# The second attention's projection as three products of rounded parts, with rows turned two tiles at a time

## The reference

```python
x = x + _L0_xattn_ref(_layernorm(x), ctx_768, ...)                  # cross attention, 8 heads
x = x + _L0_ffn_ref(_layernorm(x), ...)                             # ternary weights, 8-bit tokens, gelu
x = x + _L1_xattn_ref(ctx_768, _layernorm(x), mask_BxS2_bk0, ...)   # the second attention
x = x + _L1_ffn_ref(_layernorm(x), ...)                             # 8 experts, the best 2, and a shared one

def _L1_xattn_ref(x, latents, mask, ...):       # latents: the normed tokens
    xn = layernorm(x, ln_x_g, ln_x_b)
    ln = layernorm(latents, ln_l_g, ln_l_b)
    q = ln @ Wq.T
    kv = jnp.concatenate([xn @ Wkv.T, ln @ Wlkv.T], axis=1)
    ...                                         # rms norm of q and k per head (4 heads of 64), softmax, values, Wo
```

## Time and profile before

| what | value |
|---|---|
| runs | 929.19, 927.93, 929.03 us; median 929.03 |
| profiled execution | 928.22 us, its span 926.5 us, mean granted clock 0.987 |
| busy | PE 94%, PEld 66%, DVE 68%, ACT 57%, POOL 42% |
| FFN's tail and projection | about 126 to 195 us of the span |
| second attention, then the experts | from 195 us to the end |

### The profile page before, as it was taken

One profiled execution on the slowest core, in us unless ns is written; L12 is line 12 of the kernel. 1 busy time (PEld: TensorE's weight loads), 2 busy tenths in 40 slices (PEclk: granted clock), 3 DMA queues, 4 the chain that ended last, 5 costly groups with the idle time before them and its releaser, 6 DMA issues.

```text
span 926.5 us, 14997 instructions
## 1 busy us (share of the span) xinstructions
PE 866.8 (94%) x4299; PEld 611.3 (66%) x4300; DVE 630.7 (68%) x1275; ACT 532.6 (57%) x851; POOL 388.9 (42%) x334
## 2 busy tenths in 40 slices
PE   9977789889999999999999999999999999999992
PEld 4635455545555555555457887878888888888881
DVE  5788987855567557456488779846666666666666
ACT  2558885445665765775554534326666666666650
POOL 2144455435676746756515545512222222222210
PEclk9999999989999999999999999999999999999997
DMA  9400000009478578569565100078711298526405
GB/s 310 110 1 1 0 1 1 1 5 364 160 292 328 194 305 326 219 269 350 199 262 196 82 1 1 12 316 342 305 40 36 71 348 341 208 88 254 116 9 182
DMA packets 49909, 154.07 MB, mean 166 GB/s; under 512 B 6266, under 2 KB 24438, under 8 KB 44236
## 3 DMA queue, kind: packets, MB, share of 16 engines
q1 hardware_dynamic: 46124, 144.25, 41.4%
q0 software_dynamic: 3744, 9.31, 3.1%
HBM read 97.85 MB, written 56.62 MB: 167 GB/s over the span
## 4 chain that ended last, share of the span: by engine, by line
PE 67%; DVE 17%; ACT 6%; issue 3%; DMA 3%; POOL 2%; SPq 1%; DVEq 0%; ACTq 0%; POOLq 0%
PE banks L1047 11%; PE banks L1300 8%; PE banks L1302 8%; PE banks L1301 8%; PE banks L1015 4%; PE banks L1039 3%; PE banks L1040 3%; DVE small L2105 2%; PE banks L1337 2%; PE banks L1339 2%; PE banks L1338 2%; PE banks L1313 2%; PE banks L953 2%; PE banks L919 1%; PE banks L1061 1%
## 5 line engine op out<-in xcount | busy, mean ns | idle before, releaser
L1047 PE MATMUL banks<-wexp 128*65 128x512 f32 (+1 forms) x288 | 149.9, 602 | 3.5 <-ACT wexp L1614 3.5
L677 POOL TENSOR_TENSOR cv_hl<-wexp,cv_hl 128x1024 fp32r<-128x1024 f32 x45 | 108.6, 2421 | 56.0 <-ACT cv_hl L1591 55.4
L1300 PE MATMUL banks<-ring,x_hi 128*128 x312 | 127.5, 408 | 0.0
L1302 PE MATMUL banks<-ring,x_lo 128*128 x312 | 122.1, 391 | 0.0
L1301 PE MATMUL banks<-ring,x_hi 128*128 x312 | 122.0, 391 | 0.0
L1614 ACT ACTIVATE wexp<-banks 128x512 f32<-128x512 f32 x128 | 76.4, 599 | 64.2 <-PE banks L1040 63.8
L2105 DVE TENSOR_REDUCE small<-banks 128x1 bf16<-128x1107 f32 x64 | 84.1, 1314 | 38.4 <-PE banks L1015 38.4
L1750 ACT ACTIVATE banks<-wexp 128x1024 f32 x72 | 73.5, 1021 | 47.7 <-DVE aux L2496 47.7
L1728 ACT ACTIVATE aux<-banks 128x512 f32<-128x512 f32 x78 | 46.7, 599 | 61.2 <-PE banks L1302 45.2
L1039 PE MATMUL banks<-q_hi,k_hl 128*128 128x512 f32 x144 | 76.7, 533 | 1.9 <-ACT q_lo L1582 1.0
L1302 PEld LDWEIGHTS banks<-ring,x_lo 128*128 128x128 f32 x312 | 58.6, 188 | 13.2
(11 more groups left out here) (374 smaller groups left out, 2171.5 us busy)
## 6 DMA issues: line engine op xcount, KB each, us to landing
wsplit<-cv_hl SPq DMA_DIRECT2D x45, 1024.0 KB, 8.0
ring<-wsplit SPq DMA_DIRECT2D x32, 1280.0 KB
wexp<-in_L_ffn_w SPq DMA_DIRECT2D x40, 512.0 KB, 5.9
wexp<-in_expert_biases SPq DMA_DIRECT2D x8, 1152.0 KB, 6.6
ring<-wsplit SPq DMA_DIRECT2D x4, 1024.0 KB, 8.2
wexp<-moe_y SPq DMA_DIRECT2D x7, 512.0 KB, 6.1
wexp<-in_L_ffn_sw SPq DMA_DIRECT2D x5, 512.0 KB, 9.0
x_sb<-in_x SPq DMA_DIRECT2D x4, 512.0 KB, 7.6
```

The lines of the kernel that those rows point to most:

```text
L677: g.tensor_tensor(sides(hl[:, PIECE:2 * PIECE]), raw, sides(hl[:, 0:PIECE]).bitcast(f32), ALU.subtract).then_inc(s['cv_lo'], 1)
L1047: mm(pb[5 + half][0:DA, :], vh[b][0:w, c, :], pT[q % 3][0:w, :], start=c == 0, stop=c == len(KTILES) - 1).then_inc(s['a_pv'], 1)
L1300: mm(o[:], x_hi[u][:, kc, :], hi, start=kc == 0 and not primed, stop=False, skip_group_check=primed)
L1302: last = mm(o[:], x_lo[u][:, kc, :], hi, start=False, stop=primed and kc == KC - 1, skip_group_check=primed)
```

## The change

1. The projection is three products of rounded parts. New buffers l_hi, l_lo (256 inner x 4 tiles) and w_hi, w_lo (256 x 768), over space that the experts' weight conversion uses later. ACT copies the weights to w_hi once, before the FFN's turn -3 (128x1536); POOL forms w_lo in two pieces of 128x768, in its FFN loop at t = 7 and t = 9. PE issues per tile 6 products of 512 and 6 of 256 columns in place of 4 float32 products.
2. Rows are turned in pairs p of tiles (2p, 2p+1): `proj_in(p)` is 4 transposes, `proj_T(p)` 4 activations of 128x256 (2 to l_hi, then 2 to xnT), and DVE has a new `proj_low(p)` (128x512: xnT - l_hi). The pair's parts must be there before the third product of its first tile.
3. `proj_in(p+1)` and `proj_T(p+1)` come behind tile 2p. `proj_in(p)` waits for `proj_tokens(2p+1)`.
4. The roots of tiles 8 to 15: DVE aggregates before t = 0 (`late_variances`), ACT takes the root after its table load, DVE refines it at t == 2 (`norm`, 6 operations).
5. Semaphores f_pre and warm are renamed or joined with others.

```diff
@@ POOL, FFN loop @@
                 g.tensor_scalar(xn[:, t % 2, :], x_sb[:, t, :], mv[:, t, 0:1], rstd[:, t:t + 1], ALU.subtract, ALU.mult).then_inc(s['f_xn'], 1)
+                if t in W_LOW_AT:
+                    pool.wait_ge(s['w_pre'], 3)
+                    kc = W_LOW_AT.index(t)
+                    g.tensor_tensor(w_lo[:, kc, :], wT[:, kc, :], w_hi[:, kc, :].bitcast(f32), ALU.subtract).then_inc(s['w_pre'], 1)
@@ PE @@
-            def proj_in(t):
-                pe.wait_ge(s['l_xh'], t + 1)
-                if t > 0:
-                    pe.wait_ge(s['l_xT'], t)
+            def proj_in(p):
+                pe.wait_ge(s['l_xh'], 2 * p + 2)
+                if p > 0:
+                    pe.wait_ge(s['l_xT'], 2 * p)
                 for kc in range(KC):
-                    last = tr(pb[7][:, kc * P:(kc + 1) * P], xn[:, t % 4, kc * P:(kc + 1) * P], ident[:])
+                    for u in range(2):
+                        at = (kc * 2 + u) * P
+                        last = tr(pb[7][:, at:at + P], xn[:, (2 * p + u) % 4, kc * P:(kc + 1) * P], ident[:])
                 last.then_inc(s['l_xT_full'], 1)
 
             def proj_part(t, k):
+                p = t // 2
                 if k == 0:
-                    pe.wait_ge(s['l_xT'], t + 1)
+                    if t == 0:
+                        pe.wait_ge(s['w_pre'], 2 + 1 + KC)
+                    pe.wait_ge(s['l_xT'], 2 * p + 1)
                     if t >= 2:
                         pe.wait_ge(s['l_qk'], t - 1)
                 a, n = ((0, 2 * D), (2 * D, D))[k]
+                o, at = pb[PROJ_BANK[t % 2] + k][:, 0:n], slice(t % 4 * P, (t % 4 + 1) * P)
                 for kc in range(KC):
-                    last = mm(pb[PROJ_BANK[t % 2] + k][:, 0:n], xnT[:, kc, t % 4 * P:(t % 4 + 1) * P], wT[:, kc, a:a + n], start=kc == 0, stop=kc == KC - 1)
+                    mm(o, l_hi[:, kc, at], w_hi[:, kc, a:a + n], start=kc == 0, stop=False)
+                    mm(o, l_hi[:, kc, at], w_lo[:, kc, a:a + n], start=False, stop=False)
+                if k == 0:
+                    pe.wait_ge(s['l_xlo'], p + 1)
+                for kc in range(KC):
+                    last = mm(o, l_lo[:, kc, at], w_hi[:, kc, a:a + n], start=False, stop=kc == KC - 1)
                 if k:
                     last.then_inc(s['l_qkv'], 1)
 
             def proj(t):
                 proj_part(t, 0)
                 proj_part(t, 1)
-                if t + 2 < T:
-                    proj_in(t + 2)
+                if t % 2 == 0 and t + 2 < T:
+                    proj_in(t // 2 + 1)
@@ ACT @@
+            def proj_T(p):
+                act.wait_ge(s['l_xT_full'], p + 1)
+                if p >= 2:
+                    act.wait_ge(s['l_qkv'], 2 * p - 2)
+                for to in (l_hi, xnT):
+                    for kc in range(KC):
+                        last = a(to[:, kc, pair_at(p)], pb[7][:, kc * 2 * P:(kc + 1) * 2 * P], ACT.Identity,
+                                 scale=lg[:, kc:kc + 1], bias=lb[:, kc:kc + 1])
+                    last.then_inc(s['l_xT'], 1)
...
                 a(qkv[:, t, :], banks[:, o:o + QKV], ACT.Copy).then_inc(s['l_qk'], 1)
-                if t + 2 < T:
-                    proj_T(t + 2)
+                if t % 2 == 0 and t + 2 < T:
+                    proj_T(t // 2 + 1)
...
                 if i == -4:
                     keep_context(1)
+                    act.wait_ge(s['ld_l1'], NLD['ld_l1'])
+                    a(flat(w_hi), flat(wT), ACT.Copy).then_inc(s['w_pre'], 1)
...
             ready(ACT.Sqrt)
+            root(LN_EARLY, T)
@@ DVE @@
+            def proj_low(p):
+                ve.wait_ge(s['l_xT'], 2 * p + 2)
+                if p >= 2:
+                    ve.wait_ge(s['l_qkv'], 2 * p - 2)
+                at = pair_at(p)
+                v.tensor_tensor(l_lo[:, :, at], xnT[:, :, at], l_hi[:, :, at].bitcast(f32), ALU.subtract).then_inc(s['l_xlo'], 1)
+
+            def late_variances():
+                aggregate(LN_EARLY, T)
+                v.tensor_scalar(root_a[:, LN_EARLY:T], mv[:, LN_EARLY:T, 1], 1.0 + LN_EPS, LN_EPS ** 2, ALU.mult, ALU.add).then_inc(s['root_in'], 1)
...
                     for t in range(4):
                         proj_tokens(t)
-                if T - 3 < i < T:
-                    proj_tokens(i - T + 6)
+                    proj_low(0)
+                if i == T - 2:
+                    proj_low(1)
+                    for t in range(4, 6):
+                        proj_tokens(t)
+                if i == T - 1:
+                    for t in range(6, 8):
+                        proj_tokens(t)
...
+            late_variances()
             for t in range(T):
                 if t >= TB + 4:
                     maximum(0, 2 * (t - TB - 4), HEAD0_MAX)
                     maximum(0, 2 * (t - TB - 4) + 1, HEAD0_MAX)
-                if 6 <= t + 4 < T:
+                if 8 <= t + 4 < T:
                     proj_tokens(t + 4)
                 proj_squares(t)
-                if t == 3:
-                    scales(LN_EARLY, T, ln_r, 1.0 + LN_EPS, LN_EPS ** 2)
+                if t % 2 == 0 and 2 <= t < T - 2:
+                    proj_low(t // 2 + 1)
+                if t == 2:
+                    norm(LN_EARLY, T, 0.0, ln_r)
```

More of the change, by code:

```diff
@@ L137, in program @@
         _, cv_hl = aliased(("x_span0", XS), ("cv_hl", CVHL * 2 * PIECE))
+        assert KC * (2 * 4 * P + 2 * QKV) <= CVHL * 2 * PIECE
+        _, l_hi, l_lo, w_hi, w_lo = aliased(("x_span16", XS), *((n, KC * 4 * P) for n in ("l_hi", "l_lo")), *((n, KC * QKV) for n in ("w_hi", "w_lo")))
+        l_hi, l_lo, w_hi, w_lo = (v[:].rearrange("p (a b) -> p a b", a=KC) for v in (l_hi, l_lo, w_hi, w_lo))
         _, xh, xl, hb0, _, hb1, _, g_hl = aliased(("x_span6", XS + WSP), ("xh", T * D), ("xl", T * D), ("hb0", 4 * I),
@@ L388, in program, with pair_at @@
         PROJ_BANK = (2, 0)
+        W_LOW_AT = (7, 9)
+        def pair_at(p):
+            return slice(p % 2 * 2 * P, (p % 2 + 1) * 2 * P)
         LN_EARLY = TB
@@ L582, in _ @@
             g.memset(ones[:], 1.0)
-            g.memset(ones_b[:], 1.0).then_inc(s['warm'], 1)
+            g.memset(ones_b[:], 1.0).then_inc(s['const'], 1)
             link(g.memset(ident[:], 0.0))
@@ L789, in warm @@
                     mm(pb[7][:], ones_b[:], ones_b[:].unsqueeze(1).to_broadcast([P, 4, P]), start=True, stop=True)
-            pe.wait_ge(s['warm'], 1)
+            pe.wait_ge(s['const'], 2)
             warm(28)
-            pe.wait_ge(s['const'], 2)
+            pe.wait_ge(s['const'], 3)
             pe.wait_ge(s['ld_l0'], NLD['ld_l0'])
@@ L895, in _ @@
             warm(WARM_L0)
-            pe.wait_ge(s['f_pre'], 2)
+            pe.wait_ge(s['w_pre'], 2)
             def ffn_in(t, u):
@@ L967, in between @@
                     proj_in(0)
-                    proj_in(1)
                     pe.wait_ge(s['f_acc'], T - 1)
@@ L1449, in kept @@
                 last.then_inc(s['prep_free'], 1)
-            act.wait_ge(s['const'], 2)
+            act.wait_ge(s['const'], 3)
             ready(ACT.Sqrt)
@@ L1475, in signs @@
                 act.wait_ge(s['w_times'], k + 1)
-                a(flat(q), flat(raw), ACT.Sign, bias=cols[:, 32:33]).then_inc(s['f_pre'], 1)
+                a(flat(q), flat(raw), ACT.Sign, bias=cols[:, 32:33]).then_inc(s['w_pre'], 1)
             def magnitudes(k, raw, q):
@@ L1557, in between @@
                     proj_T(0)
-                    proj_T(1)
                 if T - 3 <= i < T:
@@ L1797, in _, with norm @@
             roots = [0]
-            def norm(c0, c1, guard):
+            def norm(c0, c1, guard, to=rstd):
                 ve.wait_ge(s['root_out'], roots[0] + 1)
@@ L1808, in norm @@
                 link(v.tensor_scalar(t_, t_, 0.5, guard, ALU.mult, ALU.max))
-                link(v.reciprocal(d, t_))
-            ve.wait_ge(s['const'], 2)
+                link(v.reciprocal(to[:, c0:c1], t_))
+            ve.wait_ge(s['const'], 3)
             link(v.tensor_scalar(eno_i[:], eno_i[:], 31, None, ALU.bitwise_and))
@@ L1992, in ffn_statistics @@
                 ve.wait_ge(s['f_yout'], t + 1)
-                statistics(t)
+                return statistics(t)
             def ffn_turn(i, u):
@@ L2006, in ffn_turn @@
                 if there(i - 1):
-                    ffn_statistics(i - 1)
+                    last = ffn_statistics(i - 1)
+                    if isinstance(i, int) and i == T:
+                        link(last)
                 if there(i + 4):
```

8 lines of the change are left out of this document (4 added, 4 removed).

## The result

The changed kernel takes 936.4 us (median of 4 runs, 936.31 to 936.61), the kernel before 929.01 (4 runs, 927.93 to 929.19): ratio 1.0082, 95% interval 1.0065 to 1.01: 0.8% slower, a small loss but clear of the noise. The profiled execution took 936.61, its span 934.9; before 928.22 and 926.5.

The account below looks back on a forecast made before the run. It took the stretch as mixed: PE paces tiles 0 to 6, DVE from about 147 us. Terms 3.4 + 2.5 + 2.0 + 0.6 = +8.5 us on 928.22 gave 936.7, forecast 937; range 930.5 to 941.5.

Parts of the forecast that it names:

- Products: PE's projection products: a tile takes 2.10 us instead of 2.58, so 16 tiles free 7.7 us of PE.
- First wait, the tail: FFN's tail: proj_low(0) ahead of turn 13 moves DVE's turn by 2.7 us; proj(4) starts at 146.7 instead of 144.50.
- Second wait, proj(4): PE waits inside proj(4) for proj_low(2), queued behind DVE's squares; proj(4) ends 4.0 us later, mean squares 3.4 later.
- rival 3: POOL's squares hold proj_low, or the clock falls already at the earlier stalls: 3 to 4 us more, 940.5; chance 0.14.
- Third wait, proj_in(6): PE stands 6.2 us for tokens(13), behind root_means and scaled on DVE: +2.5 us, and +2.0 for the fallen clock.
- Tiles 12 to 15: Behind the first maximum: shorter products win 0.1 us, proj_low(7) before the third maximum costs 0.7; together +0.6.
- w_hi, w_lo: ACT's weight copy and POOL's pieces fall into waiting time: counted 0; uncovered, up to 1.5 us and 2 x 1.6.
- Contention: proj_low on DVE could be held beside POOL's squares: counted 0, bounds 0 and 5 x 1.0 us.
- Rival 1: PE keeps the pace through tiles 0 to 10, pairs' parts always ready: -3.6 us, 925; chance 0.11.
- Rival 2: The clock stays up in PE's stall of 6 us at proj_in(6): +6.5 us, 935; chance 0.22.
- Rival 4: ACT's slack hides turn 13's delay; only the block at proj_in(6) and clock remain: +3.7 us, 932.5; chance 0.14.
- rival 5: No change in the whole kernel: PE's losses and gains cancel, 929 us; chance 0.06.

Follow-up runs that it names:

- after_again: The changed kernel run again with no edit, on a second chip: 936.23 us, ratio 1.0088 to the kernel before.
- tail_order: Changed kernel with proj_low(0) behind turn 13's factors and proj_T(1) behind turn 14's scaling (L1522): 936.4 us, ratio 1.0087 to the kernel before.
- low2_first: Changed kernel with proj_low(2) ahead of DVE's loop over the tiles instead of behind proj_squares(2): 938.56 us, ratio 1.0114 to the kernel before.
- low2_ctx: Changed kernel with proj_low(2) ahead of DVE's tile loop and the context's squares moved to the FFN's last turn: 935.18 us, ratio 1.0068.
- all_moves: Changed kernel with tail order, proj_low(2) and context's squares early, proj_tokens(13) ahead of root_means, 14 filling matmuls: 933.11 us, ratio 1.0041.
- pairs_f32: Changed kernel with float32 products back, pairs and late roots kept, rounded parts and proj_low removed: 933.03 us, ratio 1.0046 to the kernel before.
- fill_stall: Changed kernel with 22 unused matmuls on PE between proj(10) and proj_in(6): 931.43 us, ratio 1.0041 to the kernel before.
- tokens13_fill: Changed kernel with proj_tokens(13) ahead of root_means and scaled, plus 14 unused matmuls ahead of turned(0): 931.36 us, ratio 1.0025.
- tokens13: Changed kernel with proj_tokens(13) moved on DVE ahead of proj_squares(8), root_means and scaled: 933.12 us, ratio 1.0052 to the kernel before.

## Why the prediction was right

The forecast was 937.0, measured 936.4; the sum of 8.5 us stands against 8.4 in the profiled executions. (The median lies 0.2 us below the profiled execution, where it was taken to lie above it.) The mechanism is as forecast: the three waits stand where they were said to stand, with nearly the sizes worked out. That the sum agrees to 0.1 us is luck. The three shifts of the stretch were 3.4 up to `tokens(13)`, 4.5 for block and clock and 0.6 behind, in all 8.5. They measured 3.35, 3.95 and 0.2, in all 7.5, in the first execution and 2.06, 4.35 and 0.2, in all 6.6, in after_again. What fills the sum up, 0.9 and 1.0 us, lies outside the stretch, where the prediction had nothing. Point by point:

- **Products.** Right: six start 0.23 apart and six 0.12, and PE's busy time fell. The four activations of a pair took 1.9 us as worked out, `proj_low` 0.69 (0.68).
- **First wait, the tail.** Right in mechanism and size: hidden row of turn 13 at 133.37 ("near 133"), PE's transposes at 140.26 (140.2), `proj(4)` at 146.71 (146.7). What I had not seen is how little of it is a price of its own: with turn 13 2.6 us earlier (tail_order), `proj_low(2)` came 0.66 earlier and the median did not move.
- **Second wait, proj(4).** Right in mechanism: `proj_low(2)` at 149.06 (149.15), PE idle 2.00 us (2.25). `proj(4)` ended at about 152.3, where 151.1 was worked out, as the clock fell behind the stall, which I had as rival 3. Mean squares came 4.1 us later than before from the same origin (37.28 against 33.17), and 2.8 in after_again, where it did not fall; 3.4 was the term, which held no fall of the clock there. It lies between, so its agreement is luck: 0.6 too much without the fall, 0.7 too little with it. Nor does the shift stay as it is up to `tokens(13)`, as worked out: 0.8 of it is caught up (3.35 and 2.06 there), as DVE waits 0.93 us for POOL ahead of tile 8's squares where it waited 1.88 before.
- **Third wait, proj_in(6).** Right: worked out 2.5 for the block and 2.0 for the clock; measured 2.4 and 1.6 to 2.0. PE stood 5.43 us, not 6.2, as it was done with `proj(10)` only at 168.3 instead of 167. `tokens(13)` at 173.26 (172.8), the remainders done at 183.33 (183.4).
- **Tiles 12 to 15.** The mis-sized term: +0.6 worked out. `proj_low(7)` does stand before the third maximum, but it comes 2.55 us behind the second (186.38 to 188.93) instead of 2.22: squares and `proj_low` first fill the 0.88 us in which DVE waits for the products anyway. From the first maximum to the table load it is 20.25 us against 20.03, +0.2.
- **w_hi, w_lo.** Nothing visible: the stretch began 0.48 us later in the first execution and 0.03 in after_again.
- **Contention.** Counted at 0, and right for the forecast kernel. DVE's remainders, as one tile's instructions (duration min/median/max in ns):

```profile
L2057 DVE TENSOR_TENSOR l_lo<-aux,l_hi x8: 680/692/693, 130.4 to 188.3; 128x512 fp32r<-128x512 f32 x8
```

None of the eight was held. The small operation behind one of them took 1.01 us at 149.66 instead of about 0.17. The Trainium skill, "SBUF — State Buffer", "Who interferes with whom", lets the later of the two engines wait; the changed kernel's trace shows its cost at that small operation and at the POOL square beside this `proj_low` (1.58 us from 149.06, elsewhere 1.04), and at no `proj_low`. With the order moved it does reach one: `proj_low(3)` took 0.93 us in low2_first, low2_ctx and all_moves.

Rival 1 needed PE idle below 1.5 us between 128 and 152 us; it idled 5.7. Rival 2 (the clock stays up) fell with 0.50 from 172 us on. Of rival 3 one half came true in part, the clock that falls at `proj(4)`, in four executions of six; the time stayed 4 us below its 940.5, as nothing held `proj_low` and the stalls ahead of 139 us left the clock at 1.00. Rival 4 fell with PE's transposes at 140.26, rival 5 with the interval. By parts, in ratios to the kernel before: late roots -0.21%, pairs on top of them +0.67% (1.0046 against 0.9979), rounded parts on top of those +0.36% (1.0082 against 1.0046), in us about -2.0, +6.2 and +3.3. On the marks the pairs cost 5.6 (table load at 73.61 against 67.99): the block and its clock, 4.1 (10.32 in pairs_f32 against 6.17), and 1.5 ahead of `tokens(13)`. The rounded parts cost 3.3 or 2.4 there, against the first execution or after_again. This is the price of each part in this order of adding; rounded parts without the pairs were not run, nor pairs of float32 products with `tokens(13)` moved. The prediction had the late roots' gain inside its second wait (0.8 to 1.4 us; the marks show 1.4).

Open stays why the same stall costs the clock in one execution and not in another, and what makes the part behind the table load 729.2 us long in one execution and 731.8 in another.

## What to carry to other kernels

An engine that is busy 94% of the span need not be the bound where the change works: read stage by stage who stands still, before paying with work on the engine that is late. A step that makes another engine's input in two parts brings a wait into the middle of a queue; name what is queued behind it. A stall that is followed by another can't be priced singly: take it away and look which wait is longest next, since a long stall can cost the clock too. And where one execution of a kernel loses the clock and another does not, a mark of one profile is good to about 1 us: compare profiles in which the clock did the same.

## What the runs showed of the hardware

- The granted clock fell to 0.50 behind stalls of 1.97 to 2.00 us at `proj(4)` in four executions (changed, fill_stall, tokens13_fill, tail_order), and stayed at 1.00 behind 1.98 us at the same place in two (after_again, tokens13) and behind 2.87 us elsewhere (low2_ctx). The advice of the Trainium skill, "TensorE: Matmul & The Clock Gate", "Why this matters for your kernels", to avoid idle gaps agrees with both long stalls here, of 5.43 and 3.35 us; which of the short ones costs the clock could not be told from their length.
- The clock can fall late in the stall: in tokens13 it was still 1.00 from 168 to 170 us, with PE idle throughout, and 0.54 in the next 2 us.
- Twenty-two products without use in the place of a stall won 1.6 to 2.0 us of clock, and no cost of theirs shows: `proj_in(6)` starts 0.5 us behind `tokens(13)` with and without them.
- A DVE subtraction of 128x512 takes 0.68 to 0.69 us alone and took 0.93 beside a POOL square (low2_first); a POOL square that started together with one took 1.58 instead of 1.04 (changed).
